# One attention-and-experts block on one core: image 5 joins the one-hot dispatch, and small work changes place

## The reference, cut to what matters

```python
x: (8, 16, 16, 256)                     # 8 images of 256 tokens, 256 channels
# 1. x = x + attention(layernorm(x)): a softmax along the row and one along the column
r = softmax(q . k_row - gw * dist);  c = softmax(q . k_col - gw * dist)
out = (r . v + c . v) @ Wo.T + bo
# 2. t = t + experts(layernorm(t)): 2048 tokens, 8 experts, one expert a token, 256 places an expert
idx = argmax(softmax(x2d @ wg));  mask = one_hot(idx)
loc = cumsum(mask, axis=0) - 1          # a token's place with its expert, over all images in order
mask = mask * (loc < 256)
h = relu(dispatched[e] @ w1[e]);  eo = h @ w2[e]     # (256 x 256) @ (256 x 1024) @ (1024 x 256)
out[token] = gate * eo[expert, loc]
```

## Time and profile before

| | |
|---|---|
| median of 3 runs | 189.29 us (189.07 to 189.89) |
| the profiled execution | 190.0 us, of which the span of the trace is 188.1 |
| granted TensorE clock, mean | 0.991 |
| busy share of the span | PE 94%, DVE 76%, POOL 66%, ACT 60% |
| last chain, by engine | PE 68%, DVE 13%, ACT 7%, issue 5%, DMA 4% |

### The profile page before, as it was taken

The page is one execution under the profiler, slowest core; times in us unless marked ns, Lnnn a source line. Parts: engine busy times, 40 slices in busy tenths (PEclk is TensorE's granted clock), DMA queues, the critical chain, the costliest instruction groups (busy, mean ns, idle before and its releaser), DMA issues.

```text
span 188.1 us, 3939 instructions
## 1 busy us (share of the span) xinstructions
PE 176.8 (94%) x1370; PEld 170.0 (90%) x1370; DVE 142.9 (76%) x384; ACT 112.4 (60%) x273; POOL 123.5 (66%) x175
## 2 busy tenths in 40 slices
PE   7999999989999899979899899999999999999980
PEld 7998999989898798869899899999999999999970
DVE  0586759898796979755767879999698996997820
ACT  3257995767858487432659795791874935845000
POOL 4387465798988857628249778748367495368652
...
GB/s 170 231 370 235 288 242 237 255 94 58 56 83 61 88 51 132 257 149 307 31 311 366 252 103 371 29 100 376 57 308 138 68 333 156 215 13 44 3 68 28
DMA packets 23860, 31.66 MB, mean 168 GB/s; under 512 B 2728, under 2 KB 20649, under 8 KB 23840
## 3 DMA queue, kind: packets, MB, share of 16 engines
...
q10 hardware_dynamic: 960, 0.85, 1.4%
...
## 4 chain that ended last, share of the span: by engine, by line
PE 68%; DVE 13%; ACT 7%; issue 5%; DMA 4%; POOLq 1%; POOL 0%; DVEq 0%; ACTq 0%; SPq 0%
PE banks_v L614 7%; PE banks_v L615 7%; PE banks_v L621 6%; PE bank_pT L621 4%; PE bank_pT L614 4%; PE bank_pT L615 4%; PE bank_xT L731 4%; PE bank_q L621 3%; PE bank_q L614 3%; PE bank_q L615 3%; PE bank_s L621 3%; PE bank_s L615 3%; PE bank_s L614 3%; DMA slots<-row,slot 3%; DVE qT_low L1125 2%
## 5 line engine op out<-in xcount | busy, mean ns | idle before, releaser
L955 ACT ACTIVATE w_high<-w_in_sb 128x1024 fp32r<-128x1024 f32 x22 | 22.9, 1055 | 6.2 <-DMA w_in_sb<-in_L_ffn_w 6.2
L571 POOL DMA_INDIRECT out<-y,goal x16 | 17.1, 1068 | 11.4 <-issue 6.0
L553 POOL TENSOR_TENSOR w_low<-w_in_sb,w_high 128x1024 fp32r<-128x1024 f32 x7 | 16.8, 2412 | 10.2 <-ACT w_high L955 10.2
L553 POOL TENSOR_TENSOR w_low<-vx,w_high 128x1024 fp32r<-128x1024 f32 x8 | 20.1, 2532 | 4.8 <-ACT w_high L955 4.8
L493 POOL DMA_INDIRECT slots<-row,slot x14 | 14.3, 1022 | 10.8 <-DVE slot L1237 4.1
L1324 DVE TENSOR_TENSOR w_low<-w_in_sb,w_high 128x1024 fp32r<-128x1024 f32 x12 | 15.3, 1279 | 5.9 <-ACT w_high L955 5.9
L686 PE MATMUL banks_o<-vx,pT 128*128 128x266 f32 x64 | 16.5, 398 | 1.6 <-ACT pT L921 1.3
L614 PE MATMUL banks_v<-w_high,h_high 128*128 128x256 f32 x64 | 16.3, 291 | 0.5 <-issue 0.5
L615 PE MATMUL banks_v<-w_high,h_low 128*128 128x256 f32 x64 | 15.8, 283 | 0.0
L686 PEld LDWEIGHTS banks_o<-vx,pT 128*128 128x128 f32 x64 | 11.4, 189 | 3.7 <-ACT pT L921 1.6
L1053 ACT ACTIVATE h_high<-bank_xT 128x512 fp32r<-128x512 f32 x8 | 4.7, 593 | 16.8 <-PE bank_xT L621 16.8
...
## 6 DMA issues: line engine op xcount, KB each, us to landing
...
```

What stands on the lines that cost most here:

```text
L553: step = nc.gpsimd.tensor_tensor(w2_low[e % 2][:, half, :], w2_raw[e % 2][:, half, :], w2_high[e % 2][:, half, :].bitcast(f32), ALU.subtract)
L571: nc.gpsimd.indirect_dma_start(out_rows, bass.IndirectOffsetOnAxis(ap=goal[j][:, c:c + 1].bitcast(u32), axis=0), y[j][:, c, :], None, boun ...
L955: nc.scalar.activation(high[e % 2][:, half, :], raw[:, half, :], ACT.Copy).then_inc(ready, 1)
```

## The change

Image 5 now goes by one-hot products as well (`EARLY` is 5, not 6). The early load takes place after image 4's scatter. `onehot_5` lies in `xs[1]`, `xn_5` in `y[1]`. TensorE makes dispatch_5, counts(7), dispatch_6, dispatch_early, dispatch_7, in this order, and the warm products are left out. GpSimd scatters images 5, 6 and 7 after the early load: six indirect DMAs.

In the setup VectorE makes var_eps and minus_mean for images 0 to 4; for 5 to 7 they stay with GpSimd. `pre_residual` and `sum_marks` have one operation less (TensorE's counts one product more), `second_w1_low` moves from turns 3, 4, 5, 6 to 4, 5, 6, 6, and `x_and_bias(i)` waits for the marks of image i-2. ScalarE's `normalised_x` moves behind `query`. Among the first experts VectorE makes w2's last piece ahead of xg_low(0), and `output_rows(0)` behind `gathered_low(2)`.

```diff
-EARLY = B - 2
+SETUP_GROUPS = 5
+EARLY = B - 3
+W1_LOW = {4: (0,), 5: (1,), 6: (2, 3)}
...
-            sp.wait_ge(x2_ready, 2 * EARLY)
-            sp.dma_start(out_view[:, tiles(EARLY - 1), :], row[1][:, :, 0:D]).then_inc(x2_stored[1], 16)
+            for i in (last, EARLY):
+                sp.wait_ge(x2_ready, 2 * i + 2)
+                sp.dma_start(out_view[:, tiles(i), :], row[i % 2][:, :, 0:D]).then_inc(x2_stored[i % 2], 16)
             sp.wait_ge(w1_split, 2)
             sp.dma_start(w1_in_sb[:, :, :], w1_view[2]).then_inc(w1_in, 16)
-            for j in range(2):
-                sp.wait_ge(row_sent[j], 32 * (EARLY // 2))
+            sp.wait_ge(x2_stored[last % 2], 16 * (last // 2 + 1))
+            sp.sem_inc(row_free, 1)
+            sp.wait_ge(row_sent[last % 2], 32 * (last // 2 + 1))
+            sp.sem_inc(row_free, 1)
+            sp.wait_ge(row_sent[1 - last % 2], 32 * (EARLY // 2))
             sp.dma_start(sl_early, slots_view[:, 0, :, :]).then_inc(early_in, 16)
...
-                norm.mark(nc.gpsimd.tensor_scalar(var_eps[:, a:b], mean_var[:, a:b, 1], 1.0, EPS_C, ALU.mult, ALU.add))
-                norm.done(nc.gpsimd.tensor_scalar(minus_mean[:, a:b], mean_var[:, a:b, 0], -1.0, 0.0, ALU.mult, ALU.add))
+                if g >= SETUP_GROUPS:
...
                 pool.wait_ge(xT_high_ready, min(i + 2, B))
+                wait(pool, chosen_ready, i - 1)
...
-                if i in W1_TURNS:
-                    second_w1_low(i - W1_TURNS[0])
-                scatter_rows(i - 2)
+                for n in W1_LOW.get(i, ()):
+                    second_w1_low(n)
+                if i < B - 1:
+                    scatter_rows(i - 2)
+                else:
+                    pool.wait_ge(placed_5, 1)
+                    for t in range(2):
+                        nc.gpsimd.tensor_scalar(onehot_5[:, t, :], place_row, place_of[2][:, t:t + 1], None, ALU.is_equal).then_inc(onehot_5_ready, 1)
...
             pool.wait_ge(early_in, 16)
+            scatter_rows(EARLY)
             scatter_rows(B - 2)
             scatter_rows(B - 1)
...
-            keep_warm(WARM_TAIL, ps_pT)
+            def dispatch_5(t):
+                pe.wait_ge(xn_5_ready, t + 1)
+                pe.wait_ge(onehot_5_ready, t + 1)
+                for c in range(DC):
+                    nc.tensor.matmul(ps_x0[c], xn_5[:, t, chunk[c]], onehot_5[:, t, :], start=t == 0, stop=False)
...
+            dispatch_5(0)
+            dispatch_5(1)
+            counts(B - 1)
             dispatch_6(0)
-            counts(B - 1)
             dispatch_6(1)
+            dispatch_early()
             dispatch_7(0)
             dispatch_7(1)
-            dispatch_early()
...
-                if i + 2 < B:
-                    normalised_x(i + 2)
                 transposed_prob(i - 1)
                 exponentials(i)
                 query(i + 1)
+                if i + 2 < B:
+                    normalised_x(i + 2)
...
+                if g < SETUP_GROUPS:
+                    setup.done()
+                    nc.vector.tensor_scalar(minus_mean[:, a:b], mean_var[:, a:b, 0], -1.0, None, ALU.mult).then_inc(var_ready, 1)
+                    nc.vector.tensor_scalar(var_eps[:, a:b], mean_var[:, a:b, 1], EPS_C, None, ALU.add).then_inc(var_ready, 1)
...
             first_w2_piece(2)
+            first_w2_piece(3).then_inc(first_w2_low, 1)
...
             hidden_low(0, [0])
-            first_w2_piece(3).then_inc(first_w2_low, 1)
             hidden_low(0, [1, 2, 3])
...
-            output_rows(0, 2)
             hidden_low(1, [2])
             gathered_low(2)
+            output_rows(0, 2)
```

More of the change, by code:

```diff
@@ L165, in build @@
         mean_var = sb("mean_var", [P, NT, 2])
-        var_eps, minus_mean, rstd, nmr, std = (sb(n, [P, NT]) for n in ("var_eps", "minus_mean", "rstd", "nmr", "std"))
+        var_eps, rstd, nmr, std = (sb(n, [P, NT]) for n in ("var_eps", "rstd", "nmr", "std"))
+        mean_token = sb("mean_token", [P, NT, 2])
+        minus_mean = mean_token[:, :, 0]
         xn = sb("xn", [P, 2, D])
@@ L186, in build @@
         chosen = [c[:, 1:3, :] for c in chosen_wide]
-        before = [sb(f"before{j}", [P, E], bf16) for j in range(2)]
+        before = [sb(f"before{j}", [P, 2, E], bf16) for j in range(2)]
         counted, loc = sb("counted", [P, 2, E]), sb("loc", [P, 2])
-        place_of = [sb(f"place_of{j}", [P, 2]) for j in range(2)]
+        place_of = [sb(f"place_of{j}", [P, 2]) for j in range(3)]
         slot = [sb(f"slot{j}", [P, 2], i32) for j in range(2)]
@@ L201, in build @@
         goal = [sb(f"goal{j}", [P, 2], i32) for j in range(2)]
+        onehot_5, xn_5 = xs[1], y[1]
         onehot_6, onehot_7, sl_early = y[0], h_high[1][:, 0:2, :], sl[:, 0:2, :]
@@ L435, in first_rstd @@
                 pool.wait_ge(var_ready, 2 * (g + 1))
-                norm.mark(nc.gpsimd.tensor_scalar(var_eps[:, a:b], mean_var[:, a:b, 1], 1.0, EPS_C, ALU.mult, ALU.add))
-                norm.done(nc.gpsimd.tensor_scalar(minus_mean[:, a:b], mean_var[:, a:b, 0], -1.0, 0.0, ALU.mult, ALU.add))
+                if g >= SETUP_GROUPS:
+                    norm.mark(nc.gpsimd.tensor_scalar(var_eps[:, a:b], mean_var[:, a:b, 1], 1.0, EPS_C, ALU.mult, ALU.add))
+                    norm.done(nc.gpsimd.tensor_scalar(minus_mean[:, a:b], mean_var[:, a:b, 0], -1.0, 0.0, ALU.mult, ALU.add))
                 nc.gpsimd.tensor_tensor(rstd[:, a:b], var_eps[:, a:b], minus_half[:, a:b], ALU.pow).then_inc(rstd_ready, 1)
@@ L489, in scatter_rows @@
             def scatter_rows(i):
[L490 to L491 removed]
+                if i < EARLY or i == B - 1:
+                    wait_apart(pool, slot_ready, min(i, EARLY) + 1, pool_passed)
                 for t in range(2):
@@ L511, in sum_marks @@
                 if i == 0:
-                    nc.gpsimd.tensor_tensor(b[:, :], c[:, 0, :], c[:, 1, :], ALU.add).then_inc(before_ready, 1)
-                    return
-                pre.done(nc.gpsimd.tensor_tensor(b[:, :], before[i % 2][:, :], c[:, 0, :], ALU.add))
-                nc.gpsimd.tensor_tensor(b[:, :], b[:, :], c[:, 1, :], ALU.add).then_inc(before_ready, 1)
+                    nc.gpsimd.tensor_copy(b[:, :, :], c).then_inc(before_ready, 1)
+                else:
+                    nc.gpsimd.tensor_tensor(b[:, :, :], before[i % 2][:, :, :], c, ALU.add).then_inc(before_ready, 1)
             pool.wait_ge(b_ready, 1)
@@ L519, in _ @@
             pool.wait_ge(token_in, 16)
+            pre.done(nc.gpsimd.tensor_copy(mean_token[:, :, 1], token[:, :]))
             pre_residual(0)
@@ L700, in counts @@
                     pe.wait_ge(before_ready, i - 1)
-                    nc.tensor.matmul(ps_count, ones[:, :], before[1 - i % 2][:, :].unsqueeze(1).to_broadcast([P, 2, E]), start=False, stop=False)
+                    for t in range(2):
+                        nc.tensor.matmul(ps_count, ones[:, :], before[1 - i % 2][:, t:t + 1, :].to_broadcast([P, 2, E]), start=False, stop=False)
                 nc.tensor.matmul(ps_count, upper, new[:, 1:3, :], start=False, stop=True).then_inc(count_made, 1)
@@ L799, in dispatch_6 @@
                 for c in range(DC):
-                    nc.tensor.matmul(ps_x0[c], xn[:, t, chunk[c]], onehot_6[:, t, :], start=t == 0, stop=False)
+                    nc.tensor.matmul(ps_x0[c], xn[:, t, chunk[c]], onehot_6[:, t, :], start=False, stop=False)
             def dispatch_7(t):
@@ L809, in dispatch_7 @@
                 for c in range(DC):
-                    nc.tensor.matmul(ps_x0[c], row7_low[:, t, chunk[c]], onehot_7[:, t, :], start=False, stop=False)
+                    step = nc.tensor.matmul(ps_x0[c], row7_low[:, t, chunk[c]], onehot_7[:, t, :], start=False, stop=t == 1)
+                    if t == 1:
+                        step.then_inc(x0_made, 1)
             def dispatch_early():
@@ L1010, in _ @@
             act.wait_ge(xT_made, B)
+            act.wait_ge(x2_ready, 2 * (EARLY + 1))
+            for t in range(2):
+                centred(row[1], xn_5, t).then_inc(xn_5_ready, 1)
             for t in range(2):
@@ L1272, in _ @@
             maxima(B - 1, 0)
-            place(B - 3, slot_of(B - 3)).then_inc(slot_ready, 1)
+            place(B - 3, place_of[2]).then_inc(placed_5, 1)
             maxima(B - 1, 1)
```

28 lines of the change are left out of this document (16 added, 12 removed).

## The result

The changed kernel takes 187.76 us (median of 18 runs, 187.22 to 188.36), the kernel before 189.20 (18 runs, 188.15 to 190.16): ratio 0.9918, 95% interval 0.9904 to 0.9933. That is 1.44 us less, half of the 2.9 that was forecast and inside the range. The profiled execution took 187.77, its span is 185.8.

The account below looks back on a forecast made before the run. TensorE, busy 94% of the span, was taken to lose time in the turns, the dispatch and the first two experts. -2.2 + 0.15 - 0.65 - 0.9 + 0.7 = -2.9 from 189.29 gave 186.4 us; eight in ten within 184.7 to 188.3.

Parts of the forecast that it names:

- A: Turns 3 to 6: TensorE's waits for pT (1.3) and xT_low (0.8) go, plus 0.1 inside product groups; -2.2 us.
- the first rival: Turns stay long: VectorE, or w1_low beside its two-input work in a new place, holds xT_low back; 187.7 us, chance 0.17.
- B: Setup: VectorE's var_eps and minus_mean for the first five images cost half of one image's 0.34; +0.15, bounds 0 and +0.5.
- C: Dispatch: the early load no longer ends last, TensorE's own work does; hidden(0) at 83.85 instead of 84.50, -0.65 us.
- the rival in which it is late: Dispatch: the early load lands after 80.5 and delays what waits for it; C 0, D -0.3, 187.65 us, chance 0.06.
- D: Expert 0's output: VectorE's w2 piece moves ahead of xg_low(0), so losses of 0.53 and 0.35 go; -0.9 us.
- E: Expert 1's output: later output_rows(0) delays GpSimd's scatter and w_low, so TensorE stands until about 111.8; +0.7 us.
- The clock: Rival: without warm products the clock falls to 1.2 GHz at hidden(0); 192.6 us, chance 0.04.
- the turns did not stay long behind the wait for `chosen`: Rival, GpSimd passes it on: x_and_bias behind `chosen` delays scatter and xb, losing A; 188.6 us, chance 0.07.

Follow-up runs that it names:

- m12: The changed kernel with GpSimd's w1_low pieces back in turns 3, 4, 5, 6, one each, the wait for `chosen` kept: 187.02 us, ratio 0.9882.
- m13: The kernel before with only the joined small operations of pre_residual and sum_marks and one product more in counts: 187.32 us, ratio 0.9914.
- m15: The changed kernel with one-input slot and ratio, setup back on GpSimd, output_rows(0) in its old place, and the old dispatch: 186.03 us, ratio 0.9842.
- m7: The changed kernel keeping only the new dispatch and joined small operations, its other edits put back as before the change: 187.31 us, ratio 0.9910.

## Why the prediction was right

**A, turns, -2.2.** Measured -2.16 (-0.70, -0.60, +0.17, -1.03 by turns): the size was right, the reasons only in part. It was put down to xn's place (1.3) and to the meeting in turn 6 (0.8). The runs give the joined small operations 1.24 alone, xn's place 0.59 beside them, and the wait for `chosen` 1.3 in turn 6 where w1_low is placed as before. These overlap, since a turn in which TensorE hardly waits takes some 7.3 already; the first rival took 0.6 to 0.8 in turn 5 as well (8.08, with 7.49 in m12), so that the size came out right by compensation, which is luck. The step that failed: GpSimd's small operations were named without a term of their own, though taking them out alone moved x_and_bias off `chosen` in turn 6 (0.99) and brought nmr sooner in turn 4 (0.41).

**The first rival**, w1_low meeting VectorE's two-input operations in a new place, happened: in turns 4, 5 and 6. It had been priced inside the turns; its larger part fell into the tail of image 7 (+0.55), a stage for which the forecast has no term. In m12, with the pieces spread again, 0.41 of it goes in the turns and 0.50 in the tail.

**B, +0.15.** About +0.34, within its bounds.

**C, -0.65.** The stage came out at 6.20, against 6.2 said. But the 6.83 from which it was reckoned was one execution: 6.28 in the second. Of the difference between 2.2 by profiles and 1.44 by medians up to 0.55 lies there. The step that failed was to take 4.72 and 3.29, two DMA times of one execution, as the kernel's: in m13 the same two took 3.64 and 2.83, in m15 4.04 and 3.61. That they make the kernel before vary by 2 us is not shown. The early load had landed at 75.97, where 76.8 was reckoned, though it took 5.5 and not 3.29; the rival in which it is late is out. What no run confirms is the gain itself at the median: m7 with the dispatch and m13 without it took the same.

**D, -0.9.** hidden(0) to its output fell by 0.70, and the slow pairs behind it by 0.19 (6.60 to 6.41 from expert 0's output to the next hidden product): -0.89. With the piece in its old place and six scatters (m7) the first is 6.61, so 0.55 is the piece's place there. But m13, with the piece in its old place and four scatters, has 6.08 for the first and 6.74 for the second, together 12.82 against 13.36 before, 13.19 in m7 and 12.47 here. There GpSimd's w_low starts 2.87 after hidden(0) instead of 3.67 (88.17 and 84.50 in the earlier trace rows), and VectorE is free again before expert 0's output starts. So what the old place costs depends on when GpSimd starts. The w2 piece was not undone alone.

**E, +0.7.** The wait for w_low was there as forecast, 0.98; +0.33 in this profile, 0.56 to 0.69 in the others with y late.

**The clock** stayed at 1.00 without the warm products, and the turns did not stay long behind the wait for `chosen`: these two rivals are out.

Sum by the profiles, against -2.9: 0.24 in B, 0.55 in the tail, 0.04 in A, 0.02 in C, less 0.17 in D and E, gives -2.22. The rest to -1.44 is the first profile's distance from its median, of which the dispatch's 0.55 is shown; the remainder, 0.2, is open. Against the second profile of the kernel before (188.68) the changed one gains 0.9; the 1.44 of the medians lies between the two.
